# Narrow attention of a fused decoder: score products in tiles of 32 rows, eight side by side, in one four-bank buffer instead of two two-bank buffers

## The chip, the core and the metric

The kernel is one program on one NeuronCore of a Trainium2 chip. The metric is the device time of the whole program in microseconds, median of several executions. TensorE (PE in the profile) multiplies into PSUM, VectorE (DVE) and ScalarE (ACT) read PSUM and work on SBUF, GpSimd (POOL) works on SBUF only, and SyncE (SP) issues most transfers. The engines run side by side and wait for each other only through semaphores; each works through its own instructions in program order.

## The reference, cut to what matters

Two decoder layers over x of 64 batches x 64 tokens x 128 channels; only the first two of six parts matter here, the "narrow" attentions with 16 heads of 8 channels:

```python
x = x + _L0_attn_ref(_layernorm(x), W_qkv, W_proj)              # causal self-attention
x = x + _L0_xattn_ref(_layernorm(x), ctx_1024, ctx_1024, ...)   # cross-attention, with biases
# each: scores = q_head . k_head (8 channels), softmax over 64 keys, times v, then a projection
```

After them come a mixture of 8 experts, a wide attention, a single-head cross-attention and a quantised feed-forward part.

## The kernel before, in words

`narrow_attention_phase` is the first of five phases. A *unit* is 128 tokens, that is two batches of 64. Four units (UB = 4) make a *block*, and 8 blocks (NB = 8) cover x once. Blocks 0 to 7 are self-attention and blocks 8 to 15 cross-attention on the same rows, so there are 64 items (block, unit).

Scores. TensorE can't multiply one head of 8 channels by itself without a matmul for each head. So the keys of a block are *spread*: `spread_k` (line 352) writes KX, where for head slot h the transposed keys are kept only in the 8 channel rows of that head and are zero elsewhere (a multiplication by the mask `of_head`). With 128 channel rows taken as two halves of 64 rows, a half holds 8 heads, and one matmul of a 64-row, 64-column tile gives the scores of 64 queries against 8 heads x 64 keys = 512 columns. `scores` (line 429) does this for two batches b and two halves r, four tiles of 64x64 in all, which write `bank[rows[b], r, :]`: two banks of 512 fp32 for each item. The buffers `S_ps[0]` and `S_ps[1]` take turns, four banks in all. In self-attention four bf16 matmuls of the same shape first write the causal mask (line 446), and the fp32 score matmuls (line 451, recorded as two pieces each) add to it.

Softmax of an item: DVE `subtract_max` (lines 760 and 764) reads the 1024 scores of each partition twice, once for the maximum of each head and once to subtract it into E. ACT `exponentials` (line 657). PE `transpose_e` (line 461) turns E into `ET_ps`, ACT `evacuate_e` (line 665) copies it, PE `weigh_values` (line 474) multiplies by V, DVE `normalise_o` (lines 773 and 777) divides by the sums.

The order of each engine is written out by hand in its `step(blk, ...)`, four slots u = 0 to 3, each for one unit. The scores of an item are issued two slots ahead of its `weigh_values` (LAG = 2), its transpose one slot ahead. So in step(blk) PE does

- slot 0: scores of unit 2 of this block, `project_q` of the next block (416), `transpose_e`, `weigh_values`, `project_v` (425)
- slot 1: scores of unit 3, `turn_o` (482; it waits until ACT has written V of the next block, line 621), `transpose_e`, `weigh_values`, `project_o` (488)
- slot 2: scores of unit 0 of the next block, `transpose_e`, in late cross blocks `turn_x2` (495), `weigh_values`
- slot 3: scores of unit 1 of the next block, in late cross blocks `logits` (502), `transpose_x` (403) and `transpose_e` of unit 0, `weigh_values`, `project_k` (412)

Below, S0 to S3 are the score products of units 0 to 3. DVE has in its slot 2, ahead of `subtract_max` of unit 0, `add_residual` (818, it needs `project_o`) and `normalise` (752). On POOL `spread_k` takes eight instructions for a block (four in block 0, where DVE's `spread_half`, line 788, takes the other four).

What sets when scores may be written, in `scores`:

```python
                if later(blk, 1) or u >= 2:
                    wait_here(pe, d_ready, n_ - 1, passed)
                bank = S_ps[u % 2]
```

`d_ready` counts the items whose subtraction (line 764) is done. Item n_ is thus written once item n_ - 2 is subtracted, and the two buffers let PE be one item ahead of DVE.

The prologue of PE is: `transpose_x(0)`, `project_k(0)`, `project_q(0)`, `project_v(0)`, scores of units 0 and 1, `transpose_x(1)`, `project_k(1)`, `transpose_e` of unit 0. ACT's prologue has the copy of the second block's keys (601) ahead of the first two exponentials.

Of the kernel before, what the change touches and what calls it, by code (L numbers as in the profile page):

```python
# [7 lines left out]
P = 128  # L8
B, T, C = 64, 64, 128
NU = B * T // P  # L10
H = 16
D0 = C // H
# [7 lines left out]
ALU = mybir.AluOpType  # L20
ACT = mybir.ActivationFunctionType
AX = mybir.AxisListType
# [44 lines left out]
def wait_here(eng, sem, value, passed):  # L67

    eng.wait_ge(sem, value)
    eng.sem_inc(passed, 1)  # L70
# [44 lines left out]
def narrow_attention_phase(nc, k):  # L115

    UB = 4
    NB = NU // UB
    ALL = 2 * NB
    BB = 2 * UB  # L120
    TOK = UB * P
    HALF = H // 2
    PAIRS = H // 2
    LAG = 2
    NE = 8
# [2 lines left out]
    with ExitStack() as ctx:  # L128
        def sb(name, shape, dt=F32):
            return ctx.enter_context(nc.sbuf_tensor(f"n_{name}", shape, dt))  # L130

        def ps(name, shape):
            return ctx.enter_context(nc.psum_tensor(f"n_{name}_ps", shape, F32))
# [16 lines left out]
        temp = sb("temp", [P, 1])  # L150
        qscale = sb("qscale", [P, 1])
        qbias = sb("qbias", [P, 1])
        of_head = sb("of_head", [P, HALF])
        ctxT = sb("ctxT", [P, 2, TOK])
        stats = sb("stats", [P, UB, 6])
        mv = sb("mv", [P, UB, 2])
# [5 lines left out]
        QT = sb("QT", [P, 2, TOK])  # L162
        KT = sb("KT", [P, TOK])

        KX = sb("KX", [P, 2, BB, HALF * T])

        VB = sb("VB", [P, 2, BB * PAIRS, VW])
        row_max = sb("row_max", [P, 2, H])
# [2 lines left out]
        rsum = sb("rsum", [P, H])  # L171
        O = sb("O", [P, 2, UB, C])
        OT = sb("OT", [P, TOK])
        S_ps = [ps(f"S{i}", [P, 2, 512]) for i in range(2)]
        ET_ps = ps("ET", [P, PAIRS * P])
        PV_ps = ps("PV", [P, 512])
        G_ps = ps("G", [P, 512])
# [62 lines left out]
        N_WEIGHTS = (5, 10)  # L240

        block = ctx.enter_context(nc.Block())

        looped = [False]

# [38 lines left out]
        def later(number, least):  # L284

            return not isinstance(number, int) or number >= least
# [52 lines left out]
        @block.gpsimd  # L339
        def _(pool):  # L340
            def power(nb):
                pool.wait_ge(var_ready, nb + 1)
                nc.gpsimd.tensor_tensor(rstd[:], var_eps[:], minus_half[:], ALU.pow).then_inc(rstd_ready, 1)

            def power2(nb):
                i = nb - NB
                pool.wait_ge(var2_ready, i + 1)
                if i >= 1:
                    pool.wait_ge(xn2_ready, i)
                nc.gpsimd.tensor_tensor(rstd2[:], var2_eps[:], minus_half[:], ALU.pow).then_inc(rstd2_ready, 1)  # L350

            def spread_k(nb, p):

                if later(nb, 2):
                    pool.wait_ge(s_ps, (nb - 1) * UB)
                wait_here(pool, kT_ready, nb + 1, passed)
                src = KT[:].rearrange("c (b t) -> c b t", t=T)
                heads = range(HALF // 2) if isinstance(nb, int) and nb == 0 else range(HALF)
                for h in heads:
                    last = nc.gpsimd.tensor_scalar(KX[:, p, :, h * T:(h + 1) * T], src, of_head[:, h:h + 1], 1.0,  # L360
                                                   ALU.mult, ALU.mult)
                last.then_inc(kx_ready, 1)
# [36 lines left out]
        def _(pe):  # L399
# [29 lines left out]
            def scores(blk, u, p):  # L429

                n_ = blk * UB + u
                cross = is_cross(blk)
                if u == 0:
                    pe.wait_ge(kx_ready, blk + 1)
                    if isinstance(blk, int) and blk == 0:
                        pe.wait_ge(causal_ready, 2)
                        pe.wait_ge(kx_halved, 1)
                    pe.wait_ge(qT_ready, blk + 1)
                if later(blk, 1) or u >= 2:
                    wait_here(pe, d_ready, n_ - 1, passed)  # L440
                bank = S_ps[u % 2]
                rows = [slice(64 * r, 64 * r + 64) for r in range(2)]
                if not cross:
                    for b in range(2):
                        for r in range(2):
                            nc.tensor.matmul(bank[rows[b], r, :], k.causal_queries[rows[r], 0:T], k.causal_keys[rows[r], :],
                                             start=True, stop=False)
                for b in range(2):
                    for r in range(2):
                        at = 2 * u + b  # L450
                        mm = nc.tensor.matmul(bank[rows[b], r, :], QT[rows[r], p, at * T:(at + 1) * T],  # L451
                                              KX[rows[r], p, at, :], start=cross, stop=True)
                mm.then_inc(s_ps, 1)

            def transpose_e(blk, u):
# [35 lines left out]
            def turn_x2(i, p, bank):  # L491

                pe.wait_ge(xn2_ready, i + 1)
                for u in range(UB):
                    mm = nc.tensor.transpose(bank[:, u * P:(u + 1) * P], xn2[:, p, u, :], k.ident[:])
                mm.then_inc(x2T_ps, 1)
# [76 lines left out]
                        project_k(blk + 2, p, rel + 2)  # L573

            def epilogue():
                turn_x2(NB - 2, 0, S_ps[0][:, 0, :])
                pe.wait_ge(l_ready, NB - 2)
                turn_o(ALL - 1, 1)
                logits(NB - 2, S_ps[0][:, 1, :])
                project_o(ALL - 1)  # L580
                turn_x2(NB - 1, 1, S_ps[1][:, 0, :])
                logits(NB - 1, S_ps[1][:, 1, :])

            run_loops(pe, prologue, step, epilogue)

# [1 line left out]
        def _(act):  # L587
# [130 lines left out]
                        normalise2(blk - 1)  # L718

            def epilogue():  # L720
                evacuate_x2T(ALL - 2, S_ps[0][:, 0, :])
                evacuate_oT(ALL - 1)
                keep_logits(ALL - 2, S_ps[0][:, 1, :])
                normalise2(ALL - 1)
                evacuate_x2T(ALL - 1, S_ps[1][:, 0, :])
                keep_logits(ALL - 1, S_ps[1][:, 1, :])

            run(act, prologue, step, epilogue)

# [1 line left out]
        def _(dve):  # L731
# [24 lines left out]
            def subtract_max(blk, u):  # L756
                n_ = blk * UB + u
                dve.wait_ge(s_ps, n_ + 1)
                src = S_ps[u % 2][:].rearrange("p r (j t) -> p (r j) t", t=T)
                nc.vector.tensor_reduce(row_max[:, u % 2, :], src, AX.X, ALU.max).then_inc(max_done, 1)  # L760
                dve.wait_ge(max_done, n_ + 1)
                if later(blk, 1) or u >= 2:
                    dve.wait_ge(et_ps, n_ - 1)
                nc.vector.tensor_tensor(E[:, u % 2, :].rearrange("p (j t) -> p j t", t=T), src,  # L764
                                        row_max[:, u % 2, :].unsqueeze(2).broadcast_to([P, H, T]),
                                        ALU.subtract).then_inc(d_ready, 1)

            def normalise_o(blk, u, p):
# [13 lines left out]
            def spread_half(nb):  # L782

                dve.wait_ge(kT_ready, 1)
                dve.wait_ge(weights[0], 16 * N_WEIGHTS[0])
                src = KT[:].rearrange("c (b t) -> c b t", t=T)
                for h in range(HALF // 2, HALF):
                    last = nc.vector.tensor_scalar(KX[:, 0, :, h * T:(h + 1) * T], src, of_head[:, h:h + 1], None, ALU.mult)
                last.then_inc(kx_halved, 1)

# [1801 lines left out]
def constants():  # L2592

    t = np.arange(T)
# [21 lines left out]
        "c_cos": np.tile(np.cos(angle), (4, 1)).astype(np.float32),  # L2616
        "c_sin": np.tile(np.sin(angle), (4, 1)).astype(np.float32),

        "c_of_head": (np.arange(P)[:, None] % 64 // D0 == np.arange(H // 2)[None, :]).astype(np.float32),
    }  # L2620


# [50 lines left out]
```

## Time and profile before

| | us |
|---|---|
| median of 3 runs | 1155.99 (1155.08 to 1156.0) |
| the profiled execution, whole | 1161.69 |
| its span, first to last instruction | 1159.90 |
| narrow attention in it | about 0 to 339 |

Busy in the span: PE 997.4 us (86%), weight loads 801.9, DVE 845.9 (73%), ACT 589.2 (51%), POOL 564.1 (49%). A row of the timeline reads: start, duration, engine, line, operation, output <- inputs, number of instructions merged, and in brackets the idle time ahead of it with the instruction that ended it. Matmuls are pipelined, so the end of one row overlaps the start of the next; what an operation costs PE is the distance from its start to the start of the next one. The page says of itself that matmul ends are modelled.

### The profile page before, as it was taken

The page shows a single profiled execution, that of the slowest core. Times are in us where ns is not written, and L with a number is a line of the kernel's source. Part 1 is how long each engine was busy: PE and PEld are TensorE (multiplying, and loading weights), DVE is VectorE, ACT ScalarE, POOL GpSimd, SP SyncE. Part 2 cuts the span into 40 slices and gives each one's busy share as a digit, 9 for nine tenths or more (in the row PEclk, how much of TensorE's full clock was granted, in tenths as well). Part 3 has the DMA queues.
Part 4 walks back from the last instruction along what each step waited for, and adds up shares of the span by engine and source line. Part 5 has one row for each costly group of instructions (what it writes and reads, how often), then busy time and mean ns, then how long its engine had stood idle before and what let it go on. Part 6 is the DMA issues. An engine that isn't in the chain of part 4 may idle for free. (4 is left out here: it accounts for less than half of the span.)

```text
span 1159.9 us, 38655 instructions
## 1 busy us (share of the span) xinstructions
PE 997.4 (86%) x14756; PEld 801.9 (69%) x14759; DVE 845.9 (73%) x2025; ACT 589.2 (51%) x983; POOL 564.1 (49%) x705
## 2 busy tenths in 40 slices
PE   5999999999945799999947999999999999776454
PEld 2666666667642799999936888888888888654113
DVE  4878787888749244444328999999999998488576
ACT  3665656677720466666612444444444444356545
POOL 4332424353300433333226888888888887433104
PEclk9999999999955799999978999999999999856555
DMA  7200000000000111111130000000000000050002
GB/s 240 114 2 0 2 11 20 20 19 27 11 28 0 40 47 48 48 48 47 39 109 13 13 12 11 11 11 9 11 11 11 11 7 1 17 127 24 1 0 73
DMA packets 36984, 37.60 MB, mean 32 GB/s; under 512 B 7142, under 2 KB 31145, under 8 KB 36522
## 3 DMA queue, kind: packets, MB, share of 16 engines
q1 hardware_dynamic: 31690, 27.33, 7.7%
q0 software_dynamic: 4352, 8.92, 3.0%
q8 instruction: 48, 0.79, 0.3%
q10 hardware_dynamic: 866, 0.33, 0.1%
q14 instruction: 28, 0.23, 0.1%
HBM read 27.65 MB, written 8.91 MB: 32 GB/s over the span
## 5 line engine op out<-in xcount | busy, mean ns | idle before, releaser
L1283 POOL DMA_INDIRECT e_x<-xn_rows,e_where x72 | 68.4, 950 | 167.2 <-DVE e_where L1264 119.4
L360 POOL TENSOR_SCALAR n_KX<-n_KT,n_of_head 128x512 f32<-128x512 f32 x124 | 84.1, 700 | 123.1 <-ACT n_KT L601 86.3
L1253 DVE COPY e_y<-e_Y_ps 128x128 f32<-128x128 f32 x72 | 21.0, 292 | 112.4 <-PE e_Y_ps L1220 105.9
L760 DVE TENSOR_REDUCE n_row_max<-n_S_ps 128x16 f32<-128x1024 f32 x64 | 78.2, 1221 | 28.2 <-PE n_S_ps L451 28.1
L1440 POOL TENSOR_TENSOR a_E<-a_E,a_rsum 128x512 f32<-128x512 f32 x64 | 66.7, 1042 | 56.0 <-DVE a_rsum L1804 56.0
L665 ACT ACTIVATE n_ET<-n_ET_ps 128x1024 f32<-128x1024 f32 x64 | 65.5, 1024 | 46.6 <-PE n_ET_ps L461 45.8
L461 PEld LDWEIGHTS n_ET_ps<-ident,n_E 128*128 128x128 f32 x512 | 57.1, 142 | 34.9 <-issue 20.1
L764 DVE TENSOR_TENSOR n_E<-n_S_ps,n_row_max 128x1024 f32<-128x1024 f32 x64 | 78.4, 1225 | 2.9
L1210 PE MATMUL e_G_ps<-e_xT,e_gate_here 128*128 128x128 f32 x576 | 78.5, 281 | 0.9 <-ACT e_up_here L1173 0.9
L1688 ACT ACTIVATE a_OT<-a_VQ_ps 128x512 f32<-128x512 f32 x64 | 38.2, 597 | 78.4 <-PE a_VQ_ps L1584 78.4
L1220 PE MATMUL e_Y_ps<-m_down_w,e_hT 128*128 x576 | 76.7, 275 | 1.1 <-issue 0.8
L1210 PE MATMUL e_U_ps<-e_xT,e_up_here 128*128 128x128 f32 x576 | 77.6, 279 | 0.0
L461 PE MATMUL n_ET_ps<-ident,n_E 128*128 128x128 f32 x512 | 68.3, 276 | 8.1 <-ACT n_E L657 8.1
L657 ACT ACTIVATE n_E<-n_E 128x1024 f32<-128x1024 f32 x64 | 67.2, 1052 | 14.2 <-DVE n_E L764 14.2
L1210 PEld LDWEIGHTS e_G_ps<-e_xT,e_gate_here 128*128 128x128 f32 x576 | 72.3, 197 | 1.1 <-ACT e_up_here L1173 1.1
L474 PEld LDWEIGHTS n_PV_ps<-n_VB,n_ET 128*64 128x64 f32 x2048 | 65.3, 138 | 10.5 <-issue 10.5
L1184 ACT ACTIVATE e_silu<-e_G_ps 128x512 f32<-128x512 f32 x72 | 43.0, 597 | 58.3 <-PE e_G_ps L1210 48.1
L1210 PEld LDWEIGHTS e_U_ps<-e_xT,e_up_here 128*128 128x128 f32 x576 | 71.7, 196 | 0.0
L474 PE MATMUL n_PV_ps<-n_VB,n_ET 128*64 128x18 f32 x2048 | 71.7, 213 | 0.0
L1220 PEld LDWEIGHTS e_Y_ps<-m_down_w,e_hT 128*128 128x128 f32 x576 | 70.2, 192 | 1.8 <-issue 1.8
L1674 ACT ACTIVATE a_E<-a_E 128x512 f32<-128x512 f32 x64 | 40.2, 629 | 61.1 <-DVE a_E L1793 61.1
L1596 PEld LDWEIGHTS a_Y_ps<-a_wo,a_OT 128*128 128x128 f32 x512 | 66.6, 193 | 4.7 <-ACT a_OT L1688 1.2
(278 smaller groups left out, 2672.4 us busy)
## 6 DMA issues: line engine op xcount, KB each, us to landing
slot_out<-e_y SPq DMA_DIRECT2D x72, 64.0 KB
X<-in_x SPq DMA_DIRECT2D x8, 256.0 KB, 5.8
n_ctxT<-in_ctxT SPq DMA_DIRECT2D x8, 256.0 KB, 3.0
m_gate_w<-in_L_ffn_gate_w SPq DMA_DIRECT2D x1, 2048.0 KB, 7.5
m_up_w<-in_L_ffn_up_w SPq DMA_DIRECT2D x1, 2048.0 KB, 11.9
m_down_w<-in_L_ffn_down_w SPq DMA_DIRECT2D x1, 2048.0 KB, 17.7
xn_rows<-n_xn SPq DMA_DIRECT2D x8, 256.0 KB
t_ctxT<-in_ctxT SPq DMA_DIRECT2D x8, 256.0 KB
```

What stands on the lines that cost most here:

```text
L360: last = nc.gpsimd.tensor_scalar(KX[:, p, :, h * T:(h + 1) * T], src, of_head[:, h:h + 1], 1.0, ALU.mult, ALU.mult)
L461: mm = nc.tensor.transpose(ET_ps[:, j * P:(j + 1) * P], E[:, u % 2, j * P:(j + 1) * P], k.ident[:])
L474: mm = nc.tensor.matmul(PV_ps[64 * b:64 * b + 64, j * VW:(j + 1) * VW], ET[:, u % 2, j * P + b * T:j * P + (b + 1) * T], VB[:, p, (2 * u + ...
L657: nc.scalar.activation(E[:, u % 2, :], E[:, u % 2, :], ACT.Exp, scale=1.0 if is_cross(blk) else float(D0) ** -0.5).then_inc(e_ready, 1)
L665: nc.scalar.activation(ET[:, u % 2, :], ET_ps[:], ACT.Copy).then_inc(et_ready, 1)
L760: nc.vector.tensor_reduce(row_max[:, u % 2, :], src, AX.X, ALU.max).then_inc(max_done, 1)
L764: nc.vector.tensor_tensor(E[:, u % 2, :].rearrange("p (j t) -> p j t", t=T), src, row_max[:, u % 2, :].unsqueeze(2).broadcast_to([P, H, T] ...
L1210: mm = nc.tensor.matmul(out[:, c * P:(c + 1) * P], w[:, p, c * P:(c + 1) * P], xT[:, p, :], start=True, stop=True)
L1220: mm = nc.tensor.matmul(Y_ps[p][:, 0:C], hT[:, p, c * P:(c + 1) * P], down_w[:, bass.ds(e * F + c * C, C)], start=(c == 0), stop=(c == FC ...
L1283: nc.gpsimd.indirect_dma_start(out=x[:, j, :], out_offset=None, in_=k.xn_rows, in_offset=bass.IndirectOffsetOnAxis(ap=where[:, j, :], axis ...
L1440: nc.gpsimd.tensor_tensor(e, e, rsum[:, g % 2, :].unsqueeze(2).broadcast_to([P, GH * UB, T]), ALU.mult)\
L1596: mm = nc.tensor.matmul(Y_ps[:, u * P:(u + 1) * P], OT[:, g % 2, u, j, :], wo[:, g, j, :], start=(g == 0 and u == 0 and j == 0), stop=(g = ...
```

## The change

The channel rows are taken as four quarters of 32 rows with 4 heads each instead of two halves with 8.

- KX has 4 head slots of 64 keys instead of 8, so `spread_k` issues 4 instructions for a block instead of 8, and in block 0 POOL and DVE issue 2 each instead of 4.
- `scores` issues 8 fp32 matmuls (batch b, quarter q) of 256 columns in tiles of 32 rows x 64 columns, instead of 4 of 512 columns in tiles of 64x64. The causal mask takes 8 bf16 matmuls of 256 columns, still in tiles of 64x64, instead of 4 of 512.
- Quarter q writes the first half of bank q of one tensor `S_ps` of four banks. There is no second buffer: item n_ is written once item n_ - 1 is subtracted (`d_ready >= n_`).
- `subtract_max` reads four runs of 256 columns instead of 1024 columns in one; as many elements.
- The epilogue's `turn_x2` and `logits` use the four banks as before.

```diff
-        S_ps = [ps(f"S{i}", [P, 2, 512]) for i in range(2)]
+        S_ps = ps("S", [P, 4, 512])
...
-                heads = range(HALF // 2) if isinstance(nb, int) and nb == 0 else range(HALF)
+                heads = range(QUARTER // 2) if isinstance(nb, int) and nb == 0 else range(QUARTER)
...
-                if later(blk, 1) or u >= 2:
-                    wait_here(pe, d_ready, n_ - 1, passed)
-                bank = S_ps[u % 2]
-                rows = [slice(64 * r, 64 * r + 64) for r in range(2)]
+                if later(n_, 1):
+                    wait_here(pe, d_ready, n_, passed)
+                halves = [slice(64 * r, 64 * r + 64) for r in range(2)]
                 if not cross:
-                    for b in range(2):
-                        for r in range(2):
-                            nc.tensor.matmul(bank[rows[b], r, :], k.causal_queries[rows[r], 0:T], k.causal_keys[rows[r], :],
-                                             start=True, stop=False)
+                    for q in range(4):
+                        for b in range(2):
+                            nc.tensor.matmul(S_ps[halves[b], q, 0:QUARTER * T], k.causal_queries[halves[q % 2], 0:T],
+                                             k.causal_keys[halves[q % 2], 0:QUARTER * T], start=True, stop=False)
                 for b in range(2):
-                    for r in range(2):
+                    for q in range(4):
                         at = 2 * u + b
-                        mm = nc.tensor.matmul(bank[rows[b], r, :], QT[rows[r], p, at * T:(at + 1) * T],
-                                              KX[rows[r], p, at, :], start=cross, stop=True)
+                        heads = slice(32 * q, 32 * q + 32)
+                        mm = nc.tensor.matmul(S_ps[halves[b], q, 0:QUARTER * T], QT[heads, p, at * T:(at + 1) * T],
+                                              KX[heads, p, at, :], start=cross, stop=True)
...
-                src = S_ps[u % 2][:].rearrange("p r (j t) -> p (r j) t", t=T)
+                src = S_ps[:, :, 0:QUARTER * T].rearrange("p q (j t) -> p q j t", t=T)
...
-                for h in range(HALF // 2, HALF):
+                for h in range(QUARTER // 2, QUARTER):
```

## Rows read from the trace of the kernel before

**Rows 1.** The page: PE's granted clock in tenths, 40 slices of 29 us.

```profile
PEclk9999999999955799999978999999999999856555
```

**Rows 2.** Busy time by stage: one self-attention step (PE, loads, DVE, ACT, POOL, clock).

```profile
92.06:110.87 18.81, 18.24 (x261) 12.16 (x260) 14.94 (x30) 11.50 (x15) 6.36 (x9) 1.00 0.00 0
```

**Rows 3.** Timeline of PE in that step, from S1 on (start, us, line).

```profile
95.33 0.41 PE L446 MATMUL n_S_ps<-causal_keys,causal_queries 64*64 64x512 bf16 x4
95.56 1.03 PE L451 MATMUL n_S_ps<-n_KX,n_QT 64*64 64x512 f32 x8
96.52 0.66 PE L403 MATMUL n_G_ps<-ident,n_xn 128*128 128x128 f32 x4
97.63 1.09 PE L461 MATMUL n_ET_ps<-ident,n_E 128*128 128x128 f32 x8 [0.45 <-ACT n_E L657]
...
99.69 1.12 PE L412 MATMUL n_G_ps<-n_xnT,n_wk 128*128 128x512 f32 x2
...
101.94 1.13 PE L416 MATMUL n_G_ps<-n_xnT,n_wq 128*128 128x512 f32 x2
...
107.28 0.66 PE L482 MATMUL n_G_ps<-ident,n_O 128*128 128x128 f32 x4
```

**Rows 4.** Timeline of DVE in that step: subtraction of unit 0, then units 1 and 2.

```profile
95.26 1.23 DVE L764 TENSOR_TENSOR n_E<-n_S_ps,n_row_max 128x1024 f32<-128x1024 f32 x1
...
96.89 1.22 DVE L760 TENSOR_REDUCE n_row_max<-n_S_ps 128x16 f32<-128x1024 f32 x1
...
102.09 1.23 DVE L760 TENSOR_REDUCE n_row_max<-n_S_ps 128x16 f32<-128x1024 f32 x1 [1.70 <-PE n_S_ps L451]
```

**Rows 5.** Timeline of ACT in that step: the values of the next block.

```profile
106.01 1.22 ACT L621 ACTIVATE n_VB<-n_G_ps 64x512 f32<-64x512 f32 x2
```

**Rows 6.** Timeline of PE in a late cross-attention step, from S1 to `project_q`.

```profile
266.28 1.09 PE L451 MATMUL n_S_ps<-n_KX,n_QT 64*64 64x512 f32 x8
267.30 1.06 PE L502 MATMUL n_G_ps<-n_rw,n_x2T 128*128 128x8 f32 x8
268.21 1.07 PE L461 MATMUL n_ET_ps<-ident,n_E 128*128 128x128 f32 x8
...
271.01 1.12 PE L412 MATMUL n_G_ps<-n_ctxT,n_wk 128*128 128x512 f32 x2 [0.25 <-ACT n_xnT L592]
...
273.08 1.12 PE L416 MATMUL n_G_ps<-n_xnT,n_wq 128*128 128x512 f32 x2
```

**Rows 7.** Timeline of the same cross step: DVE's subtraction of unit 0, ACT's key copy.

```profile
265.75 1.23 DVE L764 TENSOR_TENSOR n_E<-n_S_ps,n_row_max 128x1024 f32<-128x1024 f32 x1
...
272.17 0.69 ACT L599 ACTIVATE n_KT<-n_G_ps,n_bk 128x512 f32<-128x512 f32 x1 [0.40 <-PE n_G_ps L412]
```

**Rows 8.** Timeline of the prologue, PE and DVE.

```profile
8.46 1.09 PE L403 MATMUL n_G_ps<-ident,n_xn 128*128 128x128 f32 x4 [8.46 <-DVE n_xn L752]
...
10.33 2.05 PE L412 MATMUL n_G_ps<-n_xnT,n_wk 128*128 128x512 f32 x2 [0.78 <-ACT n_xnT L592]
...
13.04 2.99 DVE L788 TENSOR_SCALAR n_KX<-n_KT,n_of_head 128x512 f32<-128x512 f32 x4 [4.72 <-ACT n_KT L601]
...
18.16 1.92 PE L451 MATMUL n_S_ps<-n_KX,n_QT 64*64 64x512 f32 x8
...
20.29 1.80 PE L451 MATMUL n_S_ps<-n_KX,n_QT 64*64 64x512 f32 x8
...
21.41 1.23 DVE L764 TENSOR_TENSOR n_E<-n_S_ps,n_row_max 128x1024 f32<-128x1024 f32 x1
22.02 0.66 PE L403 MATMUL n_G_ps<-ident,n_xn 128*128 128x128 f32 x4
...
26.12 1.09 PE L461 MATMUL n_ET_ps<-ident,n_E 128*128 128x128 f32 x8 [1.63 <-ACT n_E L657]
```

**Rows 9.** Groups by shape of the narrow phase: a DVE read with a four-dimensional pattern.

```profile
L777 DVE TENSOR_TENSOR n_O<-n_PV_ps,n_rsum 128x128 f32<-128x128 f32 x64 | 18.7, 292 | 2.2
```

**Rows 10.** Timeline of PE in an early cross step: the longest wait there.

```profile
210.53 1.09 PE L461 MATMUL n_ET_ps<-ident,n_E 128*128 128x128 f32 x8 [1.18 <-ACT n_E L657]
```

More of the change, by code:

```diff
@@ L121, in narrow_attention_phase @@
     TOK = UB * P
-    HALF = H // 2
+    QUARTER = H // 4
     PAIRS = H // 2
@@ L152, in narrow_attention_phase @@
         qbias = sb("qbias", [P, 1])
-        of_head = sb("of_head", [P, HALF])
+        of_head = sb("of_head", [P, QUARTER])
         ctxT = sb("ctxT", [P, 2, TOK])
@@ L163, in narrow_attention_phase @@
         KT = sb("KT", [P, TOK])
-        KX = sb("KX", [P, 2, BB, HALF * T])
+        KX = sb("KX", [P, 2, BB, QUARTER * T])
         VB = sb("VB", [P, 2, BB * PAIRS, VW])
@@ L242, in narrow_attention_phase, with last_bank @@
         block = ctx.enter_context(nc.Block())
+        def last_bank(q):
+            return S_ps[:, q]
         looped = [False]
@@ L575, in epilogue @@
             def epilogue():
-                turn_x2(NB - 2, 0, S_ps[0][:, 0, :])
+                turn_x2(NB - 2, 0, last_bank(0))
                 pe.wait_ge(l_ready, NB - 2)
                 turn_o(ALL - 1, 1)
-                logits(NB - 2, S_ps[0][:, 1, :])
+                logits(NB - 2, last_bank(1))
                 project_o(ALL - 1)
-                turn_x2(NB - 1, 1, S_ps[1][:, 0, :])
-                logits(NB - 1, S_ps[1][:, 1, :])
+                turn_x2(NB - 1, 1, last_bank(2))
+                logits(NB - 1, last_bank(3))
             run_loops(pe, prologue, step, epilogue)
@@ L720, in epilogue @@
             def epilogue():
-                evacuate_x2T(ALL - 2, S_ps[0][:, 0, :])
+                evacuate_x2T(ALL - 2, last_bank(0))
                 evacuate_oT(ALL - 1)
-                keep_logits(ALL - 2, S_ps[0][:, 1, :])
+                keep_logits(ALL - 2, last_bank(1))
                 normalise2(ALL - 1)
-                evacuate_x2T(ALL - 1, S_ps[1][:, 0, :])
-                keep_logits(ALL - 1, S_ps[1][:, 1, :])
+                evacuate_x2T(ALL - 1, last_bank(2))
+                keep_logits(ALL - 1, last_bank(3))
             run(act, prologue, step, epilogue)
@@ L758, in subtract_max @@
                 dve.wait_ge(s_ps, n_ + 1)
-                src = S_ps[u % 2][:].rearrange("p r (j t) -> p (r j) t", t=T)
-                nc.vector.tensor_reduce(row_max[:, u % 2, :], src, AX.X, ALU.max).then_inc(max_done, 1)
+                src = S_ps[:, :, 0:QUARTER * T].rearrange("p q (j t) -> p q j t", t=T)
+                nc.vector.tensor_reduce(row_max[:, u % 2, :].rearrange("p (q j) -> p q j", q=4), src, AX.X, ALU.max).then_inc(max_done, 1)
                 dve.wait_ge(max_done, n_ + 1)
@@ L763, in subtract_max @@
                     dve.wait_ge(et_ps, n_ - 1)
-                nc.vector.tensor_tensor(E[:, u % 2, :].rearrange("p (j t) -> p j t", t=T), src,
-                                        row_max[:, u % 2, :].unsqueeze(2).broadcast_to([P, H, T]),
+                nc.vector.tensor_tensor(E[:, u % 2, :].rearrange("p (q j t) -> p q j t", q=4, t=T), src,
+                                        row_max[:, u % 2, :].rearrange("p (q j) -> p q j", q=4).unsqueeze(3)
+                                        .broadcast_to([P, 4, QUARTER, T]),
                                         ALU.subtract).then_inc(d_ready, 1)
@@ L2617, in constants @@
         "c_sin": np.tile(np.sin(angle), (4, 1)).astype(np.float32),
-        "c_of_head": (np.arange(P)[:, None] % 64 // D0 == np.arange(H // 2)[None, :]).astype(np.float32),
+        "c_of_head": (np.arange(P)[:, None] % 32 // D0 == np.arange(H // 4)[None, :]).astype(np.float32),
     }
```

## The prediction

> **What bounds the kernel now.** The change touches only the narrow phase, so I read the stage table first. A self-attention step takes 18.81 us, in which PE is busy 18.24, DVE 14.94, ACT 11.50 and POOL 6.36 [rows 2]. PE is thus the engine to look at, but its ends are modelled, so I went through its timeline start to start [rows 3]. PE runs without a gap except in two places. It waits 0.45 us for the exponential of unit 0 before `transpose_e` at 97.63 [rows 3], and a little for V before `turn_o`: the copy ends at 106.01 + 1.22 = 107.23 [rows 5] and `turn_o` starts at 107.28 [rows 3], which also shows that a wait costs about 0.05 us after its releaser ends. Reading DVE's timeline beside it shows why: unit 0 comes late on DVE, behind `add_residual` and `normalise`, and its subtraction ends at 95.26 + 1.23 = 96.49 [rows 4]. For unit 2, DVE itself waits 1.70 us for the product [rows 4]. So the step is one ring: subtraction of unit 0, PE's work up to `project_o`, the residual, and round again. Late cross steps are similar, with one more wait, PE's `project_k` for ACT (0.25) [rows 6].
>
> **The price of a score product.** In a cross step the product starts at 266.28 and the next operation at 267.30, so it costs 1.02 us [rows 6]. The part of it that streams columns I get from the two clock levels: the same eight pieces took 1.92 us in the prologue at the lower level, where the first key projection took 2.05 against 1.12 later [rows 3, 8], and 1.09 at the upper [rows 6]. Halving the clock added 0.83, so about 0.83 of the 1.02 streams and 0.19 is start and drain. The four tiles of 64x64 take their 512 columns side by side (eight pieces of the shape of one lie within 1.09 us). Eight tiles of 32x64 with 256 columns each, side by side, need half the streaming: 0.42 + 0.19 = 0.61. In self-attention the mask costs 95.56 - 95.33 = 0.23 and the product 96.52 - 95.56 = 0.96 [rows 3]. The mask's tiles have as many columns in all, so 0.23 stays. The product now has another tile shape than the mask ahead of it. The price of a change of shape is 1.02 - 0.96 = 0.06, as the cross product follows a matmul of another shape and the self product one of its own. That gives 0.23 + 0.06 + (0.96 - 0.42) = 0.83; I take 0.90, since 16 pieces and 16 loads are twice as many, against 1.19 before. Bounds: 0.77 if the shape change costs nothing, 1.25 if eight tiles are no faster than four; for cross 0.55 and 1.08. The Trainium skill, TensorE: Matmul & The Clock Gate, section Measured speedup vs the span model, gives four row tiles 3.07 times the speed of one, not 4; by that factor the product would stream 0.54 instead of 0.42 and the whole would be some 2.5 us later. No row here has four row tiles.
>
> **The new wait.** Before, S1 (the product of unit 1) started at 95.33, though unit 0 was subtracted only at 96.49. Now it must wait until 96.49 + 0.05 = 96.54, and PE stands idle since nothing can pass it: behind it in PE's order are `transpose_x`, `transpose_e` of unit 0, `weigh_values` and `project_k`. The other three products have slack: unit 1 is subtracted at 96.89 + 1.25 + 1.23 = 99.37 and S2 starts at 99.69 + 1.06 = 100.75 [rows 3, 4]; unit 2 is subtracted at 102.09 + 1.26 + 1.23 = 104.58 and S3 starts at 105.89, some 1.4 us ahead of `turn_o` at 107.28 [rows 3, 4]. The slack is over 1 us each, more than the 0.3 saved. The Trainium skill, Perfetto Trace Analysis, section Matmuls, says that independent groups should rotate through PSUM banks so that evacuation overlaps the next group. It speaks against this change; the rows agree at one product in four only, as at the others PE has other work between.
>
> **A self step laid out again.** S1 starts at 96.54 (+1.21), ends at 97.44. `transpose_x` (0.66 less its overlap, 0.55) ends at 97.99, and `transpose_e` of unit 0 starts there instead of at 97.63: +0.36, as the old 0.45 wait for the exponential is filled. The +0.36 holds up to S2. S2 costs 0.29 less, so `project_q` starts at +0.07, at 102.01. Its other condition, the copied keys, is met: `project_k` at 99.69 + 0.36, copy 1.16 later, 0.69 long at most, gives 101.95 [rows 3, 6, 7]. From there the path to `turn_o` leads over ACT (transpose of unit 1, its copy, exponential of unit 2, V copy), so S3's saving is lost in `turn_o`'s wait for V. Behind it come `project_o` and the residual. S0's saving is lost in S1's wait. So the step is longer by 0.05 to 0.07, and **1.2 us taken from PE in each step give nothing**. Seven such steps: +0.4 (with 0.77 for a product -1.2, with 1.25 some +5).
>
> **A late cross step.** Unit 0 is subtracted at 265.75 + 1.23 = 266.98 [rows 7], S1 runs from 267.03 to 267.64, `logits` (0.91) to 268.55, and `transpose_e` starts at +0.34 against 268.21 [rows 6]. `project_k` at 271.35, key copy at 1.16 later and 0.69 long, `project_q` at 273.25 against 273.08: +0.17. The same again after it. Four such steps: +0.7 (bounds +0.4 and +3.0). Three earlier ones have no `logits`, and the exponential is waited for by 1.18 us [rows 10], which hides S1's delay; S2's saving counts up to the key copy, -0.17 each: -0.5. The last two steps: -0.4, one product's saving, between 0 and -0.8. Sum of all steps: **+0.2**, between -2.5 and +8.
>
> **DVE and POOL.** DVE reads as many elements with one more dimension in the pattern. A read of four dimensions with 128 elements takes 292 ns [rows 9], in line with 1225 for 1024 (about 1.04 ns for each further element), so nothing is added; if it were 0.05 on both reads, unit 0's chain would pay 0.1 in each of 15 steps, +1.5. `spread_k` loses half of POOL's work, most of its 6.36 us for a step [rows 2]; nobody on the ring waits for it, so it is worth 0. SP's queue and the transfers stay as they are.
>
> **The prologue.** Here the wait is bare. S0's product starts at 18.16 at the lower clock and took 1.92; now 1.92 - 0.83 + 0.06 = 1.15, end 19.3. DVE is free by then, as `spread_half` loses two of its four instructions in 2.99 us [rows 8] and everything behind it moves up 1.4. Maximum 19.4, subtraction ends 1.25 + 1.23 = 2.48 later, 21.88 (before: 21.41 + 1.23 = 22.64). S1, before at work right behind S0 (20.29, 1.80 long), starts only at 21.93. PE has been idle for 2.6 us by then. Before, it worked without a break up to 22 and its rows are at the upper level from there: `transpose_x` 0.66 at 22.02 against 1.09 at 8.46 [rows 8]. I expect the lower level to stay: mask 0.47, 0.06, streaming 0.83 and 0.10 put `transpose_x` at 23.39, +1.37. From it to `transpose_e` of unit 0 it took 26.12 - 22.02 = 4.10; the lower clock adds 0.43 in it and 2.05 - 1.12 = 0.93 in `project_k` [rows 3, 8]: +2.73 at the first `transpose_e`. Then work comes without a gap, at half speed until the clock rises. No row shows how long; before, the rise came after about 6 us of unbroken work, and half of 4 us is lost: +2.0 (0 to 3.5). Prologue: **+4.7**, between +2.7 and +6.2; with the upper level at S1 it is 21.93 + 0.90 = 22.83, **+0.8**.
>
> **The sum.** 4.7 + 0.2 = +4.9 us. The profiled execution of before took 1161.69 with a span of 1159.90; I expect 1166.6 and 1164.8. The median of the runs lies 5.7 lower: 1155.99 + 4.9 = **1160.9**.
>
> **Rivals.**
> (A) The clock has risen when S1 comes, or rises soon: prologue +0.8 to +1.5, all +1.0 to +1.7: 1157.3. For it: PE kept the upper level over idle times of 1.6 and 1.18 us [rows 8, 10]. Against: in the prologue the level had not been reached yet. Chance 0.25.
> (B) Eight tiles don't go side by side, and a product costs what it did. Self: S1 96.54 + 1.19 + 0.55 = 98.28, +0.65, nothing back at S2: 7 x 0.65 = 4.6. Late cross: 267.03 + 1.02 + 0.91 = 268.96, +0.75 x 4 = 3.0. Prologue: S1 starts at 22.69, `transpose_x` at 24.98, +2.96 + 1.36 + 2.0 = 6.3. All +13.9: 1169.9; half of it, if they go in two groups of four, 1165. For it: twice the pieces. Against: four tiles already run side by side. Chance 0.15.
> (C) Faster: TensorE's time is what counts, and the wait is absorbed. The place is S0, S2 and S3. If the V copy and the residual follow PE down instead of holding it, a self step gains 3 x 0.29 - 0.36 = 0.5 and a cross step 3 x 0.41 - 0.34 = 0.9: 7 x 0.5 + 7 x 0.9 = 10, less 0.8 to 4.7 of the prologue: 1149 (1145 to 1153). It decides from the point where PE doesn't wait at `turn_o`. Against it speak both waits in rows 3 and 5. Chance 0.12.
> The rest, 0.03, is slower still.
>
> **How the numbers follow.** The forecast (1158.5 to 1163.5) has 0.45. A measurement of this kernel can tell about 0.2%, 2.3 us, from no change. Faster than 1153.7 is (C), 0.12. Within 0.2% is (A) and the low end of the forecast, 0.26. Slower: 0.62. The range 1154.8 to 1169.0 leaves out (C) and the upper half of (B).
>
> **What would show it.** Right: an idle time of about 1.2 to 1.5 us before the mask or product of S1 in every step, ended by DVE's L764; products of about 0.6 (cross) start to start; self steps of 18.8 to 18.9, late cross steps 0.2 longer than before; still a wait for V at `turn_o`; the first `transpose_e` at about 29. Wrong: a self step under 18.5 us (then C), products of 1 us (B), `transpose_e` at 27 with rows of the upper level (A), DVE's L760 or L764 over 1.25 us, or a difference of over 2 us behind the narrow phase, since later clock changes could fall otherwise (its clock does fall there [rows 1]).

## The result, and the profile after

| | before | after |
|---|---|---|
| median | 1155.99 (1155.08 to 1158.36, 4 runs) | 1183.70 (1182.61 to 1185.86, 4 runs) |
| ratio | | 1.0237 [1.0220, 1.0255] |
| profiled execution, its span | 1161.69, 1159.90 | 1185.86, 1184.1 |
| narrow phase, up to DVE's first work of the next one | 339.62 | 372.08 |
| the rest of the span | 820.3 | 812.0 |

Slower, as predicted, but by 27.7 us and not by 4.9; the range ended at 1169.0. The narrow phase alone is 32.5 us longer.

The page of after, sections 1 and 2. The first line stands beside PE 997.4 and POOL 564.1 of before, the second beside [rows 1].

```profile
PE 1000.3 (84%) x15396; PEld 823.9 (70%) x15399; DVE 842.0 (71%) x2023; ACT 589.4 (50%) x983; POOL 521.4 (44%) x643
...
PEclk9989989898795599999996899999999999966555
```

Half of the scores' streaming is gone, yet PE is busy for as long as before. The clock row tells why: from the third to the eleventh slice, where [rows 1] has only nines, there are now four eights and a seven among them. The same self-attention step as in [rows 2], in the table of stages (PE, loads, DVE, ACT, POOL, clock):

```profile
100.81:121.34 20.53, 18.69 (x309) 13.84 (x308) 14.75 (x30) 11.61 (x15) 3.71 (x5) 0.92 0.00 0
```

20.53 us against 18.81, and a granted clock of 0.92 against 1.00; DVE and ACT do what they did. PE's timeline of that step, from S0 on, to be laid beside [rows 3]:

```profile
100.81 0.41 PE L449 MATMUL n_S_ps<-causal_keys,causal_queries 64*64 64x256 bf16 x8
101.15 0.69 PE L455 MATMUL n_S_ps<-n_KX,n_QT 32*64 32x256 f32 x16
101.77 1.09 PE L465 MATMUL n_ET_ps<-ident,n_E 128*128 128x128 f32 x8
102.79 1.11 PE L478 MATMUL n_PV_ps<-n_VB,n_ET 128*64 128x18 f32 x32
105.38 0.41 PE L449 MATMUL n_S_ps<-causal_keys,causal_queries 64*64 64x256 bf16 x8 [1.47 <-DVE n_E L768]
105.72 0.71 PE L455 MATMUL n_S_ps<-n_KX,n_QT 32*64 32x256 f32 x16
106.36 1.12 PE L407 MATMUL n_G_ps<-ident,n_xn 128*128 128x128 f32 x4
107.27 1.91 PE L465 MATMUL n_ET_ps<-ident,n_E 128*128 128x128 f32 x8
109.12 1.35 PE L478 MATMUL n_PV_ps<-n_VB,n_ET 128*64 128x18 f32 x32
110.40 1.12 PE L416 MATMUL n_G_ps<-n_xnT,n_wk 128*128 128x512 f32 x2
```

S0 is at 100.81, S1 at 105.38. The new wait is where it was predicted, 1.47 us ahead of S1, ended by DVE's subtraction. Behind it stands what was not: `transpose_x` takes 1.12 instead of 0.66, `transpose_e` 1.91 instead of 1.04, and `weigh_values` begins slow (1.35). These are rows at the lower level of 1.2 GHz. The stretch 105.38 to 112.42 has a granted clock of 0.76. From S1's start to `project_k` it is 110.40 - 105.38 = 5.02 us; where the clock holds, it is 3.47 (below).

The same happens in all 13 steps that have an idle time of over 1 us ahead of S1, and in late cross steps it can last longer, as here (PE, beside [rows 6]):

```profile
289.81 0.69 PE L455 MATMUL n_S_ps<-n_KX,n_QT 32*64 32x256 f32 x16 [1.13 <-DVE n_E L768]
290.44 1.77 PE L506 MATMUL n_G_ps<-n_rw,n_x2T 128*128 128x8 f32 x8
292.06 1.95 PE L465 MATMUL n_ET_ps<-ident,n_E 128*128 128x128 f32 x8
```

The table of stages for the stretch from there to the next `transpose_e`:

```profile
290.44:301.21 10.77, 10.77 (x80) 7.34 (x74) 5.61 (x15) 3.66 (x6) 2.41 (x4) 0.52 0.00 0
```

The account of the narrow phase, read from the starts of the 16 `project_o`, with the forecast beside it:

| stretch | forecast | after | with three fill matmuls (below) |
|---|---|---|---|
| up to the first `project_o` | +4.7 | +5.3 | +5.5 |
| six self-attention steps | +0.4 (seven) | +10.4 | +1.0 |
| three early cross steps | -0.5 | +3.9 | -0.5 |
| four late cross steps | +0.7 | +12.1 | +1.1 |
| last two steps | -0.4 | +0.8 | +2.8 |
| sum | +4.9 | +32.5 | +9.9 |

### The profile page after: what moved, and what is told of

Read it like the earlier page. It is cut to its first block and busy times, and to the rows that moved or that the text cites. A ratio compares the mean times of both kernels' runs of the same rounds, so it can differ in the third digit from the quotient of the medians.

```text
span 1184.1 us, 39868 instructions
## 1 busy us (share of the span) xinstructions
PE 1000.3 (84%) x15396; PEld 823.9 (70%) x15399; DVE 842.0 (71%) x2023; ACT 589.4 (50%) x983; POOL 521.4 (44%) x643
## 5 line engine op out<-in xcount | busy, mean ns | idle before, releaser
L364 POOL TENSOR_SCALAR n_KX<-n_KT,n_of_head 128x512 f32<-128x512 f32 x62 | 42.1, 697 | 150.6 <-ACT n_KT L605 105.8
L465 PEld LDWEIGHTS n_ET_ps<-ident,n_E 128*128 128x128 f32 x512 | 69.5, 163 | 21.0 <-issue 15.0
L465 PE MATMUL n_ET_ps<-ident,n_E 128*128 128x128 f32 x512 | 80.4, 309 | 2.6 <-ACT n_E L661 2.6
L478 PEld LDWEIGHTS n_PV_ps<-n_VB,n_ET 128*64 128x64 f32 x2048 | 69.3, 146 | 12.7 <-issue 12.6
L478 PE MATMUL n_PV_ps<-n_VB,n_ET 128*64 128x18 f32 x2048 | 75.7, 218 | 0.0
```

Source lines behind the costliest of these rows:

```text
L465: mm = nc.tensor.transpose(ET_ps[:, j * P:(j + 1) * P], E[:, u % 2, j * P:(j + 1) * P], k.ident[:])
L478: mm = nc.tensor.matmul(PV_ps[64 * b:64 * b + 64, j * VW:(j + 1) * VW], ET[:, u % 2, j * P + b * T:j * P + (b + 1) * T], VB[:, p, (2 * u + ...
```

## The experiments

Each ratio is against the kernel before, in runs on the same chip.

**The wait by itself.** The tiles of before, but S waits for the subtraction of the item just ahead.

```diff
-                if later(blk, 1) or u >= 2:
-                    wait_here(pe, d_ready, n_ - 1, passed)
+                if later(n_, 1):
+                    wait_here(pe, d_ready, n_, passed)
```

> The kernel before with one edit: item n is written only once item n-1 is subtracted. Two buffers and the 64x64 tiles stay. Theory 1 (the idle time at S1 makes TensorE's clock fall in each step): S1 starts about 1.2 us later, the clock falls behind it as in the changed kernel (transposes of unit 0 near 1.9 us instead of 1.09), some 1.5 us a step in 13 steps, 20 us. With +0.65 in 7 self steps, +0.75 in 4 late cross steps and +6 in the prologue: about 1190. Rival (the small tiles load TensorE less, and that lets the clock fall): the clock stays up here, 1170.

Measured: 1175.64 us, ratio 1.0149 [1.0118, 1.0180]. PE's timeline in a self step:

```profile
103.43 0.41 PE L446 MATMUL n_S_ps<-causal_keys,causal_queries 64*64 64x512 bf16 x4 [1.24 <-DVE n_E L764]
103.64 1.05 PE L451 MATMUL n_S_ps<-n_KX,n_QT 64*64 64x512 f32 x8
104.63 0.66 PE L403 MATMUL n_G_ps<-ident,n_xn 128*128 128x128 f32 x4
105.12 1.04 PE L461 MATMUL n_ET_ps<-ident,n_E 128*128 128x128 f32 x8
```

PE stands for 1.24 us and `transpose_e` still takes 1.04: the clock falls in none of the 13 steps (in the prologue it is down, as in after: the first `transpose_e` takes 1.97). A self step is 19.45 us, 0.64 more than before, the 0.65 that the prediction worked out for products of unchanged length. The narrow phase is 14.1 us longer (353.69 against 339.62), where the working of rival (B) had 13.9. So my arithmetic of the wait as a delay was right, and the delay alone doesn't make the fall.

**The idle time filled.** The kernel after, with six fp32 matmuls of 128 columns (results not used) ahead of S1, then with three, then with one.

```diff
+            def fill(blk, rel, prev, routed):
...                                        # waits until G_ps is free
+                for j in range(6):         # or 3, or 1
+                    nc.tensor.matmul(G_ps[:, 0:P], k.ident[:], k.ident[:], start=True, stop=True)
...
                 for u in range(UB):
+                    if u == 3 and nxt:
+                        fill(blk, rel, prev, routed)
                     if u + LAG < UB or nxt:
                         scores(*ahead(blk, u, p, LAG))
```

> The changed kernel with six extra fp32 matmuls of 128 columns (identity by identity, result never read) ahead of S1 in each step, some 1.3 us, in the time in which PE waits for the subtraction of unit 0. Theory 1: the clock stays up in all steps, the step is 18.9 us instead of 20.5, all 20 us shorter: 1163. Rival (small tiles): the clock still falls, 1184 or a little more.

> As the run with six extra matmuls, but with three, some 0.65 us, so that about 0.8 us of idle time stays ahead of S1, as in step 0 of the changed kernel, where the clock didn't fall. Theory 1: 1163 as with six. Rival: half of the idle time removed takes away half of the loss or nothing: 1173 to 1184.

> The changed kernel with a single extra fp32 matmul ahead of S1, which leaves about 1.2 us of idle time, as in the run with the wait alone, where the clock stayed up. Theory 1: it stays up here too, 1166. Theory 2: it falls in most steps, 1180 to 1184.

Measured: six 1169.11, ratio 1.0088 [1.0066, 1.0110]; three 1166.12, 1.0058 [1.0036, 1.0081]; one 1182.93, 1.0204 [1.0168, 1.0240]. PE with six, then with three, then with one:

```profile
100.10 1.60 PE L540 MATMUL n_G_ps<-ident 128*128 128x128 f32 x12
101.65 0.41 PE L449 MATMUL n_S_ps<-causal_keys,causal_queries 64*64 64x256 bf16 x8
...
103.10 1.04 PE L465 MATMUL n_ET_ps<-ident,n_E 128*128 128x128 f32 x8
```

```profile
100.88 0.94 PE L540 MATMUL n_G_ps<-ident 128*128 128x128 f32 x6
102.42 0.41 PE L449 MATMUL n_S_ps<-causal_keys,causal_queries 64*64 64x256 bf16 x8 [0.61 <-DVE n_E L780]
...
103.87 1.04 PE L465 MATMUL n_ET_ps<-ident,n_E 128*128 128x128 f32 x8
```

```profile
103.80 0.49 PE L540 MATMUL n_G_ps<-ident 128*128 128x128 f32 x2
105.34 0.41 PE L449 MATMUL n_S_ps<-causal_keys,causal_queries 64*64 64x256 bf16 x8 [1.05 <-DVE n_E L780]
...
107.21 1.91 PE L465 MATMUL n_ET_ps<-ident,n_E 128*128 128x128 f32 x8
```

This is the test of the cause. Useless work in the idle time brings the ratio from 1.0237 to 1.0088 and 1.0058, some 17 and 21 us less. S1 still starts only behind the same subtraction (with three it waits 0.61 us more for it, with six the last useless matmul ends about then), so the products come no earlier; only the clock is kept. A self step is 18.98 us in both, against 18.87 forecast. With one fill matmul and an idle time of 1.05 in self steps the fall is back in 10 of the 13 steps, and so is the time. In three of the four late cross steps of this run an idle time of 0.56 us ahead of S1 was enough, as here, while with three fill matmuls 0.61 us in self steps and 0.74 in early cross steps cost none:

```profile
265.72 0.69 PE L455 MATMUL n_S_ps<-n_KX,n_QT 32*64 32x256 f32 x16 [0.56 <-DVE n_E L780]
...
267.73 1.95 PE L465 MATMUL n_ET_ps<-ident,n_E 128*128 128x128 f32 x8
```

The column "with three" of the table above is what the edit costs without falls in the 13 steps. Over these steps the difference to the column "after" is 24.8 us, some 1.5 us for a step in self-attention and early cross steps and 2.7 in late ones: that is the falls' price. In the whole phase it is 22.6 us, since the last two steps go the other way.

**A longer wait with the long products.** The first experiment with a memset of 500 columns on DVE ahead of unit 0's maximum.

```diff
+                if u == 0 and later(blk, 1):
+                    nc.vector.memset(scratch[:], 0.0)
                 dve.wait_ge(s_ps, n_ + 1)
```

> As the run with the wait alone (64x64 tiles, two buffers), with one more DVE instruction (a memset of 500 columns, about 0.5 us) ahead of the maximum of unit 0, so that PE's idle time ahead of S1 grows from 1.24 to about 1.75 us, longer than the 1.47 us of the changed kernel. Theory 1 (the length of the idle time): now the clock falls with the big tiles too, some 20 us on top of 6 us for the memset: 1200. Theory 2 (the small tiles take part: idle time and short products together): the clock stays up, 1182.

Measured: 1192.13, ratio 1.0294 [1.0257, 1.0332]. Two self steps of PE:

```profile
66.82 0.41 PE L447 MATMUL n_S_ps<-causal_keys,causal_queries 64*64 64x512 bf16 x4 [1.71 <-DVE n_E L767]
67.03 1.05 PE L452 MATMUL n_S_ps<-n_KX,n_QT 64*64 64x512 f32 x8
...
106.66 0.64 PE L447 MATMUL n_S_ps<-causal_keys,causal_queries 64*64 64x512 bf16 x4 [1.71 <-DVE n_E L767]
107.06 1.95 PE L452 MATMUL n_S_ps<-n_KX,n_QT 64*64 64x512 f32 x8
```

The same idle time in the same place holds the clock at 66.82 and loses it at 106.66. Five of the 13 steps have a fall. The idle time thus does it with the old tiles too, but not as often as a shorter one with the new tiles (1.05 and 1.47, a fall in every self step that had one of them). My first theory, that its length alone decides, fell here: 1.71 with the old tiles mostly holds, 1.05 with the new ones mostly doesn't.

**Is it the shape or the length of the product?** The kernel after with every score product issued twice (the second overwrites the first) and a memset of 350 columns on DVE.

```diff
                 halves = [slice(64 * r, 64 * r + 64) for r in range(2)]
+                for b in range(2):
+                    for q in range(4):
+                        at = 2 * u + b
+                        heads = slice(32 * q, 32 * q + 32)
+                        nc.tensor.matmul(S_ps[halves[b], q, 0:QUARTER * T], QT[heads, p, at * T:(at + 1) * T],
+                                         KX[heads, p, at, :], start=True, stop=True)
                 if not cross:
...
+                if u == 0 and later(blk, 1):
+                    nc.vector.memset(scratch[:], 0.0)
                 dve.wait_ge(s_ps, n_ + 1)
```

> The kernel after, with every fp32 score product issued twice (the second overwrites the first, so the output is the same) and a memset of 350 columns on DVE ahead of the maximum of unit 0. The tiles stay 32 rows by 64 columns, the product is about as long as that of the kernel before (some 1.0 us), and S1's idle time should be 1.2 to 1.4 us in self-attention steps, where 64x64 tiles kept the clock up (idle 1.24) and single products of small tiles lost it (1.05 and 1.47). Theory 'shape' (something in products of small tiles themselves lets the clock fall): transpose_e behind S1 takes 1.9 us in most steps, a self step is 21.5 us or more and the whole about 1203 us. Theory 'busy time' (the short product is what is missing, whatever its shape): transpose_e keeps to 1.1 us in most steps, a self step is about 20.2 us, and the whole 1175 to 1190 us.

Measured: 1183.70, ratio 1.0252 [1.0222, 1.0282]. PE:

```profile
110.23 0.69 PE L451 MATMUL n_S_ps<-n_KX,n_QT 32*64 32x256 f32 x16 [1.17 <-DVE n_E L777]
...
111.82 0.66 PE L408 MATMUL n_G_ps<-ident,n_xn 128*128 128x128 f32 x4
112.31 1.04 PE L472 MATMUL n_ET_ps<-ident,n_E 128*128 128x128 f32 x8
```

With small tiles, twice as many of them, and 1.17 us of idle time the clock stays up, in all steps but one; a self step is 20.71 us (20.2 expected). So nothing in a 32-row tile itself lets the clock go. What is left as the difference is how much work PE has around the idle time, and the change took that away twice: by the wait, and by the shorter products. The kernel with all products doubled and a slower DVE takes as long as the kernel after (ratio 1.0252 against 1.0237): what the short products and the faster DVE saved had been paid back by the clock in full. It doesn't tell whether the work ahead of the idle time or behind it matters.

**The order on DVE.** The maximum and subtraction of unit 0 ahead of `normalise` in slot 2, for the new and for the old tiles.

```diff
-                    if u == 2 and nxt == 2:
-                        normalise(blk + 2)
                     if u + LAG < UB or nxt:
                         subtract_max(*ahead(blk, u, p, LAG)[:2])
+                    if u == 2 and nxt == 2:
+                        normalise(blk + 2)
```

> The changed kernel with DVE's order in slot 2 changed: add_residual, then the subtraction of unit 0, then normalise (before: normalise ahead of the subtraction). Unit 0 is subtracted about 1.0 us earlier, the idle time at S1 falls from 1.47 to about 0.5 us. Theory 1: no fall of the clock (20 us), and each step about 0.7 us shorter by the saved TensorE time (10 us): 1153, with the 5 us of the prologue still lost. Rival: only the order's gain counts, 1174.

> The kernel before with DVE's new order in slot 2 (residual, subtraction of unit 0, normalise). PE's wait of 0.45 us ahead of the transpose of unit 0 goes, and nothing else: 0.4 us in each of 14 steps, 6 us less than before, ratio 0.995. It tells how much of the gain of the same order on the changed kernel (ratio 0.9955, with 5 us lost in the prologue) is the small tiles': by theory 0.7 against 0.4 us a step.

Measured: new tiles 1154.58, ratio 0.9955 [0.9942, 0.9968]; old tiles 1156.43, ratio 0.9968 [0.9952, 0.9985]. PE with the new tiles:

```profile
99.64 0.41 PE L449 MATMUL n_S_ps<-causal_keys,causal_queries 64*64 64x256 bf16 x8 [0.76 <-DVE n_E L768]
...
101.10 1.04 PE L465 MATMUL n_ET_ps<-ident,n_E 128*128 128x128 f32 x8
...
103.11 1.12 PE L416 MATMUL n_G_ps<-n_xnT,n_wk 128*128 128x512 f32 x2
```

The idle time is 0.76, the clock holds, and S1 to `project_k` is 103.11 - 99.64 = 3.47 us, the figure used above. By the ratios this edit alone brings some 33 us to the kernel after and 4 to the one before. With it a self step takes 18.27 with new tiles and 18.69 with old ones, a late cross step 18.59 and 19.26: now, with the ring's slowest link shorter, the narrow products are worth 0.4 and 0.7 us a step. The whole is only about 0.1% apart, and the narrow phase is even 1.4 us longer with new tiles (it ends at 338.02 against 336.66): they pay 6.0 us more up to the first `project_o` (58.16 against 52.11) and 2.1 in the last two steps.

**The order in the prologue.** `transpose_x(1)` and `project_k(1)` ahead of S1 instead of behind it; with the new tiles alone, with both orders, and with the old tiles and both orders.

```diff
-                for u in range(LAG):
-                    scores(0, u, 0)
+                scores(0, 0, 0)
                 pe.wait_ge(v_ready, 1)
                 transpose_x(1)
                 project_k(1, 1, None)
+                scores(0, 1, 0)
```

> The kernel after with the edit of the prologue only. Every step keeps its idle time of 1.47 us ahead of S1 and its fall of the clock, the prologue loses most of its 5.3 us. Theory (the two losses are separate, prologue 5.3, steps about 1.5 each): 4 to 6 us less than the kernel after, ratio 1.018 to 1.020. Rival (a lost clock in the prologue is also what makes the later steps lose it): the steps recover as well, ratio under 1.008.

> The changed kernel with DVE's new order and, in PE's prologue, transpose_x(1) and project_k(1) ahead of S1 instead of behind it. PE then works while it waits for the subtraction of unit 0; the first transpose of exponentials comes at about 25 instead of 29 us. Against the run with the order alone 4 to 6 us less: 1149, ratio to before 0.991. Rival: the prologue's 3 us were covered by something later, no difference.

> The kernel before with both edits of order: on DVE the normalisation of slot 2 behind the subtraction of unit 0, and in the prologue of PE the second block's transposes and keys between the scores of units 0 and 1. It is the fair counterpart of the run that has both with the small tiles (ratio 0.990). The order on DVE alone gave ratio 0.9968 here. In the prologue PE of the kernel before had no idle time behind unit 0's scores, so moving transpose_x(1) and project_k(1) ahead of S1 should give little, 0 to 2 us. Theory (the small tiles are worth 0.3 to 0.4 us in each step once no wait stands ahead of S1): ratio 0.994 to 0.997, that is some 5 us above the small tiles with both edits. Rival (the gain of that run is the order alone): ratio 0.990.

Measured: the prologue's order alone, new tiles 1177.25, ratio 1.0205 [1.0167, 1.0244]; both orders, new tiles 1148.82, ratio 0.9902 [0.9878, 0.9927]; both orders, old tiles 1154.13, ratio 0.9989 [0.9974, 1.0003]. The prologue's order alone takes the first `project_o` from 58.60 to 51.59; 7.0 us is all of the prologue's loss and some more, yet the clock goes on falling in the steps, which parts the two losses. (The narrow phase ends 8.7 us earlier than in after, 363.38; by the ratios the whole gains only 3.7, within what the two intervals leave open.) One of its steps shows how little decides (PE):

```profile
57.25 0.41 PE L449 MATMUL n_S_ps<-causal_keys,causal_queries 64*64 64x256 bf16 x8 [1.48 <-DVE n_E L768]
...
58.70 1.04 PE L465 MATMUL n_ET_ps<-ident,n_E 128*128 128x128 f32 x8
```

1.48 us idle, and no fall; the next step has 1.47 and falls. The step without takes 70.57 - 51.59 = 18.98 us between `project_o` starts, the next one 91.09 - 70.57 = 20.52. A fall costs 1.5 us in a self step. Old tiles gain nothing by this order, less than the 0.994 to 0.997 expected for both, as they had no idle time there.

**The prologue filled.** With both orders PE stood for 1.25 us ahead of the products of unit 2, and `project_q` behind them was at the lower level. Five fill matmuls go there.

```diff
                 transpose_e(0, 0)
+                pe.wait_ge(kT_ready, 2)
+                for j in range(5):
+                    nc.tensor.matmul(G_ps[:, 0:P], k.ident[:], k.ident[:], start=True, stop=True)
```

> The kernel after with both edits of order, and in the prologue five more fp32 matmuls of 128 columns (results not used) ahead of the scores of unit 2, where that run had 1.25 us of idle time and, behind it, rows at the lower level (project_q 2.08 us instead of 1.13). Theory (the idle time ahead of S2 costs the clock there): project_q at 1.13 us, and 1.5 to 2 us less than without the matmuls, about 1147 us, ratio 0.988. Rival (the prologue is at the lower level there for another reason): project_q stays at about 2 us, and the time is the same or up to 0.5 us longer.

Measured: 1145.48, ratio 0.9911 [0.9892, 0.9930]. PE of the kernel with both orders, then with the filling:

```profile
25.56 0.41 PE L449 MATMUL n_S_ps<-causal_keys,causal_queries 64*64 64x256 bf16 x8 [1.25 <-DVE n_E L768]
25.90 1.02 PE L455 MATMUL n_S_ps<-n_KX,n_QT 32*64 32x256 f32 x16
26.86 2.08 PE L420 MATMUL n_G_ps<-n_xnT,n_wq 128*128 128x512 f32 x2
```

```profile
24.23 1.28 PE L533 MATMUL n_G_ps<-ident 128*128 128x128 f32 x10
...
26.60 1.12 PE L420 MATMUL n_G_ps<-n_xnT,n_wq 128*128 128x512 f32 x2
...
302.72 1.16 PE L455 MATMUL n_S_ps<-n_KX,n_QT 32*64 32x256 f32 x16 [1.41 <-DVE n_E L771]
...
304.71 1.72 PE L465 MATMUL n_ET_ps<-ident,n_E 128*128 128x128 f32 x8
```

The fall in the prologue is gone and the first `project_o` comes 1.46 us earlier (51.65 against 53.11). But the whole is no faster: the narrow phase ends at 330.56 against 330.65. The gain is given back at 302.72, where a wait of 1.41 us, which costs no clock in the other kernel, costs it here. On one chip this kernel and its fair counterpart with old tiles are 1145.48 and 1154.13. So the narrow products, with the five fill matmuls, are worth 0.75% once the clock falls in none of the 13 steps, though 0.76 us of idle time stays ahead of S1; the traces show 5.9 us of it in the narrow phase (330.56 against 336.48).

## Why the prediction was wrong

**What held.** The place, the releaser and the size of the new wait: "an idle time of about 1.2 to 1.5 us", measured 1.47. The price of a product: cross 0.61 taken, and 265.21 - 264.59 = 0.62 measured; self 0.90 taken and 101.77 - 100.81 = 0.96 measured, of it 0.34 for the mask, for which I had 0.23 + 0.06. Eight tiles do run side by side. By an estimate from the 3.07 that the Trainium skill, TensorE: Matmul & The Clock Gate, section Measured speedup vs the span model, gives for four row tiles, the cross product would have been 0.54 + 0.19 = 0.73. The measured 0.62 doesn't agree; it goes with a factor of 4. DVE's reads didn't get longer, and of the halving of POOL's `spread_k` (84.1 us before, 42.1 after) no gain shows. The page's costliest groups:

```profile
L364 POOL TENSOR_SCALAR n_KX<-n_KT,n_of_head 128x512 f32<-128x512 f32 x62 | 42.1, 697 | 150.6 <-ACT n_KT L605 105.8
L764 DVE TENSOR_REDUCE n_row_max<-n_S_ps 128x16 f32<-128x1024 f32 x64 | 78.2, 1223 | 40.7 <-PE n_S_ps L455 40.5
```

S3's saving ended in the wait for V ahead of `turn_o`, 0.36 us in a self step and ended by ACT's L625. The prologue came as laid out, S1 at 22.07 (21.93), the first `transpose_e` at 29.23 (28.85), at the lower clock up to 34.6:

```profile
22.07 0.64 PE L449 MATMUL n_S_ps<-causal_keys,causal_queries 64*64 64x256 bf16 x8 [2.74 <-DVE n_E L768]
...
29.23 1.97 PE L465 MATMUL n_ET_ps<-ident,n_E 128*128 128x128 f32 x8 [1.63 <-ACT n_E L661]
...
32.79 2.00 PE L420 MATMUL n_G_ps<-n_xnT,n_wq 128*128 128x512 f32 x2
34.62 1.04 PE L465 MATMUL n_ET_ps<-ident,n_E 128*128 128x128 f32 x8
```

34.62 against 29.31 is +5.3, where +4.7 was said.

**The step that failed** is "A self step laid out again", and with it "A late cross step". Both laid the step out with durations of the upper level behind the new idle time, 1.2 us in the self step. Whether the clock survives it was asked for the prologue only; for the steps the clock's price was put at nothing, and no reason was given. The two waits of 1.6 and 1.18 us that the trace of before got through at the upper level [rows 8, 10] are named under rival (A) alone, for the prologue, and they had the longer products around them. The runs showed a fall behind that idle time in all 13 steps of after, 24.8 us in sum by the run with three fill matmuls. No rival had a fall in the steps, so the range couldn't hold it: "1.2 us taken from PE in each step give nothing" should have gone on with "and may cost the clock, 1.5 us each time". A bound was at hand: `transpose_x` took 1.09 in the prologue instead of 0.66 [rows 3, 8], 0.43 more, and `transpose_e` behind it has twice as many matmuls of the same shape, 0.86 more. That is 1.3 us for each of 13 steps, +17 on top of 4.9, a rival at 1178 us. Its +22 for the narrow phase would still have been too low against the measured 32.5, most of all in late cross steps, two of which took 23.7 us where a step without a fall takes 19.5.

**A smaller miss.** The last two stretches were to give 0.4 and cost 0.8 in after, and 2.8 with the three fill matmuls. In the last step, of block 15, neither `project_q` nor `project_v` stands between S2 and S3, so S3 waits too, 1.41 us:

```profile
344.53 0.69 PE L455 MATMUL n_S_ps<-n_KX,n_QT 32*64 32x256 f32 x16 [1.41 <-DVE n_E L768]
```

I had checked the slack of S2 and S3 in a full step and not in the one without a next block.

The Trainium skill, Perfetto Trace Analysis, section Matmuls, has groups rotate through PSUM banks so that evacuation overlaps the next group. The prediction let that count at one product in four. The runs agree at that one (1.47 us of waiting at S1), and at S3 of block 15 (1.41).

**What stays open.** The rest of the kernel, behind the narrow phase, is 8.3 us shorter in after (812.0 against 820.3), though nothing of it was changed. Some of it is that the two profiled executions don't lie equally far above their medians, 5.7 us before and 2.2 after; by the medians 4.8 us are left (27.7 in the whole against 32.5 in the narrow phase). Over all kernels here it lies between 810.7 and 820.3 us, without an order that I can name; the prediction listed such a difference over 2 us among the signs of its being wrong. And which work decides whether an idle time costs the clock, that ahead of it or behind it, was not tried.

## What to carry to other kernels

Before a change puts a wait in front of TensorE or makes its work there shorter, price the idle time twice: as a delay, and as a fall of the clock with the durations of the lower level behind it, in every iteration. If the clock turns out to fall, look first for the order on the releasing engine (here the subtraction ahead of the normalisation, some 33 us); where none is to be had, a few useless matmuls in the gap can pay, here 17 to 21 us. And lay out the first and the last iteration by themselves, as the cover of a buffer isn't the same there.

## What the runs showed of the hardware that I had not expected

- An idle time of 1.05 us of TensorE was enough for a fall in all four self steps that had it when the products beside it were short (0.6 us), while 1.24 us cost none with products of 1.0 us, and waits of 1.24 to 1.71 us cost it in five of 13 steps. So the length of one idle time doesn't tell: 0.56 us cost it in three of four late cross steps with one fill matmul, and 0.76 us in none of the self steps with the new order on DVE.
- The same idle time with the same instructions around it can keep or lose the clock (1.48 and 1.47 us in neighbouring steps), so a saving ahead of it can be given back by a fall later: 1.46 us in the run with the filled prologue.
- The fall can show some way behind the idle time: in after the product at 105.72 still took 0.71 us, and `transpose_x` behind it was the first at the lower level. In the run with the filled prologue the product at 302.72 was already slow (1.16).
- The granted clock of a stage doesn't show everything: in the prologue's stretch 22.07 to 34.62 of after it reads 1.00, though `transpose_e` there takes 1.97 us. The durations of known matmuls tell the level better.

```profile
22.07:34.62 12.55, 10.23 (x64) 4.54 (x65) 3.97 (x4) 4.11 (x5) 2.69 (x4) 1.00 1.01 430
```
